# Stacked Q and K rows of the attention stages filled from SBUF in twelve DMAs of eight rows

## The reference

```python
q = split_heads(x @ wq + bq); k = split_heads(c @ wk + bk); v = split_heads(c @ wv + bv)
attn = softmax(einsum('bhqd,bhkd->bhqk', q, k) / sqrt(8))
out = einsum('bhqk,bhkd->bhqd', attn, v)        # heads joined again
y = out @ wo + bo
```

## Time and profile before

| | |
|---|---|
| Median of 3 runs | 6247.15 us (6244.76 to 6252.29) |
| Span of the profiled execution | 6237.0 us |
| Stage X | 2609 to 3357 us |
| Attention of F | 3357 to 4083 us |
| Stage N | 4487 to 5284 us |
| Stage Y | 5284 to 5992 us |
| TensorE, VectorE, ScalarE, GpSimd busy | 73%, 72%, 45%, 48% of the span |
| DMA | 420.18 MB, 67 GB/s in the mean |

### The profile page before, as it was taken

How to read it: one execution, slowest core, us unless ns; L and a number is a source line. 1 busy time by engine, 2 the same in 40 slices (tenths; PEclk the granted TensorE clock), 3 DMA queues, 4 the chain that set the end, 5 groups by cost and what they waited for, 6 DMA issues and landing times. The chain is left out here.

```text
span 6237.0 us, 103921 instructions
## 1 busy us (share of the span) xinstructions
PE 4570.7 (73%) x29564; PEld 3083.8 (49%) x29564; DVE 4491.5 (72%) x8773; ACT 2792.4 (45%) x6405; POOL 2994.0 (48%) x2850
## 2 busy tenths in 40 slices
PE   5777777777777777488885888846468777678853
PEld 2333333333233333266664777745367776677731
DVE  6999999999999999677776555543456655344468
ACT  4555555555555555265663333345534333233334
POOL 6777777777777777544443111144511112111102
PEclk8988989999898999799997899968778888899965
DMA  2111111111111111144442444441243442444320
GB/s 73 58 60 60 60 60 60 60 60 60 60 60 60 59 60 58 30 78 76 78 76 52 86 87 81 81 131 55 89 75 72 81 75 56 77 76 73 72 48 27
DMA packets 319745, 420.18 MB, mean 67 GB/s; under 512 B 39955, under 2 KB 301286, under 8 KB 308710
## 3 DMA queue, kind: packets, MB, share of 16 engines
q1 hardware_dynamic: 315110, 408.16, 27.9%
q0 software_dynamic: 4352, 8.95, 0.4%
HBM read 307.46 MB, written 109.58 MB: 67 GB/s over the span
## 5 line engine op out<-in xcount | busy, mean ns | idle before, releaser
L2162 POOL TENSOR_TENSOR m_h<-m_dtu,m_Bb 128x512 f32<-128x512 f32 x1024 | 1587.2, 1579 | 234.0 <-PE bank L1797 228.2
L1797 PE MATMUL bank<-m_h,ident 128*128 128x512 f32 x2048 | 1214.4, 684 | 498.5 <-DVE m_h L2061 485.7
L1797 PEld LDWEIGHTS bank<-m_h,ident 128*128 128x128 f32 x2048 | 364.4, 207 | 1162.4 <-DVE m_h L2061 1007.0
L2055 DVE TENSOR_TENSOR_SCAN m_h<-m_dA,m_h 128x512 f32<-128x512 f32 x512 | 749.2, 1463 | 6.2 <-DVE m_sz L1988 6.2
L2061 DVE TENSOR_TENSOR m_h<-m_h,bank 128x512 f32<-128x512 f32 x1024 | 671.7, 656 | 4.9 <-DVE m_h L2055 2.7
L2055 DVE TENSOR_TENSOR_SCAN m_h<-bank,m_h 128x512 f32<-128x512 f32 x512 | 620.3, 1212 | 28.1 <-DVE m_sz L1988 11.7
L385 PE MATMUL bank<-x_pT,x_vB 128*64 128x128 f32 (+1 forms) x4096 | 583.5, 288 | 9.2 <-ACT x_ou L520 9.2
L1944 ACT ACTIVATE bank<-m_dt,m_A 128x512 f32<-128x512 f32 x512 | 352.3, 688 | 492.2 <-DVE m_h L2055 434.8
L1944 ACT ACTIVATE m_dA<-m_dt,m_A 128x512 f32<-128x512 f32 x512 | 367.2, 717 | 429.1 <-DVE m_h L2055 425.4
L385 PEld LDWEIGHTS bank<-x_pT,x_vB 128*64 128x64 f32 (+1 forms) x4096 | 466.9, 147 | 58.9 <-issue 49.3
L511 ACT ACTIVATE x_sm<-x_sm,x_nm 128x77 f32<-128x77 f32 x1024 | 353.2, 348 | 123.1 <-DVE x_nm L673 123.0
(11 more groups left out here) (425 smaller groups left out, 11010.0 us busy)
## 6 DMA issues: line engine op xcount, KB each, us to landing
m_Bb<-m_B SPq DMA_DIRECT2D x32, 4096.0 KB, 11.9
x_Ks<-x_k_parts SPq DMA_DIRECT2D x32, 462.0 KB
x_q_parts<-x_qp SPq DMA_DIRECT2D x32, 384.0 KB, 2.5
x_Qs<-x_q_parts SPq DMA_DIRECT2D x32, 384.0 KB
f_Ks<-f_k_parts SPq DMA_DIRECT2D x16, 768.0 KB
a_Ks<-a_k_parts SPq DMA_DIRECT2D x16, 768.0 KB
x_xp<-x_stage SPq DMA_DIRECT2D x32, 256.0 KB
x_Qs<-x_q_parts SPq DMA_DIRECT2D x32, 256.0 KB
```

The costliest lines, as they stand in the source:

```text
L1797: pe.matmul(banks[4 + c], ident[:], h[:, k % RING, :], start=(s == 0), stop=(s == NS - 1)).then_inc(s_ya.sem, 1)
L2055: v.tensor_tensor_scan(h[:, k % RING, :], decays[k % AHEAD], h[:, k % RING, :], 0.0, ALU.mult, ALU.add).then_inc(s_h.sem, 1)
L2162: pool.tensor_tensor(h[:, k % RING, :], dtu[:, d, c, :], Bb[:, d, s, :], ALU.mult).then_inc(s_dB.sem, 1)
```

## The change

`stack` no longer writes to DRAM. As soon as Q's low part is there (and the readers of the old stack are done) SP issues six DMAs, each of which copies one part of `qp` (128 partitions of 512 columns) into one block of eight rows of `Qs`; when K's low part is there it issues six more into `Ks`. The semaphore `s_stk` becomes two, one for Q and one for K, each complete after six DMAs. TensorE waits for both. VectorE's `high` and GpSimd's `low` now wait for the stack fills of the group before, since these read `qp`. The saves, their semaphore and the DRAM tensors are gone. `Q_ORDER` and `K_ORDER` name the part of each block; the contents of the stacks are the same.

```diff
--- before.py
+++ after.py
@@ -80,6 +80,8 @@
     kt = GB * sk
     PARTS, ROWS = 3, 6 * DH
     K_TIMES = (3, 2, 1)
+    Q_ORDER = (0, 1, 2, 0, 1, 0)
+    K_ORDER = (0, 0, 0, 1, 1, 2)
     VC = DH + (gate is None)
     VW = 8 * VC
     TURNS = NG // 2
@@ -115,9 +117,6 @@
 
         def sem(name, per=1):
             return Count(nc.alloc_semaphore(f"{tag}_{name}"), per)
-
-        dram_q = nc.dram_tensor(f"{tag}_q_parts", (2, PARTS, P, GT), BF16, kind="Internal").ap()
-        dram_k = nc.dram_tensor(f"{tag}_k_parts", (2, sum(K_TIMES), P, kt), BF16, kind="Internal").ap()
 
         w = sb("w", [P, 4, D])
         bqk = sb("bqk", [P, 2])
@@ -164,7 +163,7 @@
         s_xpfree = sem("x_used"); s_pb = sem("proj_written", NU); s_pf = sem("proj_evacuated", NU)
         s_hi = sem("hi_ready", 2); s_r1 = sem("rest1_ready", 2)
         s_mid = sem("mid_ready", 2); s_lo = sem("lo_ready", 2)
-        s_ps = sem("parts_stored", 16 * (PARTS + 1)); s_stk = sem("stack_loaded", 16 * (PARTS + 1))
+        s_stk = [sem(f"stack_loaded{t}", 16 * sum(K_TIMES)) for t in range(2)]
         s_ln = sem("front_var", 1); s_lp = sem("front_pow", 1); s_xn = sem("front_norm", 1)
         s_neg = sem("neg_ready"); s_sq = sem("squares", 2); s_ms = sem("sums_of_squares", 2); s_rt = sem("roots"); s_qn = sem("qk_normed", 2)
         s_S = sem("scores", 4); s_Sf = sem("scores_used", 4); s_nmp = sem("max_parts"); s_T = sem("max_transposed")
@@ -232,26 +231,14 @@
                     sp.dma_start(gp[:, par], gate.rearrange("(g b) t d -> g t b d", b=GB)[g]).then_inc(s_gp[par].sem, 16)
 
             def stack(g, par):
-                def save(dst, src):
-                    sp.dma_start(dst.rearrange("a p t -> p a t"), src).then_inc(s_ps.sem, 16)
-
-                def fill(stack_rows, parts):
-                    sp.dma_start(stack_rows.rearrange("p h t -> p (h t)"),
-                                 parts.rearrange("a (d h) t -> (a d) (h t)", d=DH)).then_inc(s_stk.sem, 16)
-                sp.wait_ge(s_lo.sem, s_lo.at(g, 1))
-                save(dram_q[par], qp[:, 0])
-                sp.wait_ge(s_lo.sem, s_lo.at(g, 2))
-                at = 0
-                for part, times in enumerate(K_TIMES):
-                    save(dram_k[par, at:at + times], qp[:, 1, part:part + 1, 0:kt].to_broadcast([P, times, kt]))
-                    at += times
-                sp.wait_ge(s_ps.sem, s_ps.at(g + 1))
-                sp.wait_ge(s_use.sem, s_use.at((g - 1) * GB))
-                at = 0
-                for parts in K_TIMES:
-                    fill(Qs[at * DH:(at + parts) * DH, par], dram_q[par, 0:parts])
-                    at += parts
-                fill(Ks[0:ROWS, par], dram_k[par])
+                def fill(t, stacked, at, part, n):
+                    sp.dma_start(stacked[at * DH:(at + 1) * DH, par], qp[:, t, part, 0:n]).then_inc(s_stk[t].sem, 16)
+                for t, stacked, n, order in ((0, Qs, GT, Q_ORDER), (1, Ks, kt, K_ORDER)):
+                    sp.wait_ge(s_lo.sem, s_lo.at(g, t + 1))
+                    if t == 0:
+                        sp.wait_ge(s_use.sem, s_use.at((g - 1) * GB))
+                    for at, part in enumerate(order):
+                        fill(t, stacked, at, part, n)
 
             def residual(g, par):
                 sp.wait_ge(s_store.sem, s_store.at((g - 1) * 16))
@@ -334,7 +321,8 @@
             def scores(i, lb, c):
                 b, l, q = 8 * i + lb, lb // GB, lb % GB
                 if c == 0 and q == 0:
-                    pe.wait_ge(s_stk.sem, s_stk.at(2 * i + l + 1))
+                    for t in range(2):
+                        pe.wait_ge(s_stk[t].sem, s_stk[t].at(2 * i + l + 1))
                 pe.wait_ge(s_Sf.sem, s_Sf.at(b, c + 1 - 2))
                 for h in range(4):
                     hh = 4 * c + h
@@ -623,7 +611,7 @@
 
             def high(v, ch, g, t):
                 n = (GT, kt)[t]
-                v.wait_ge(s_ps.sem, s_ps.at(g))
+                v.wait_ge(s_stk[t].sem, s_stk[t].at(g))
                 v.wait_ge(s_pf.sem, s_pf.at(g, nu[(Q, K)[t]] + 1))
                 v.tensor_copy(qp[:, t, 0, 0:n], qf[:, t, 0:n]).then_inc(s_hi.sem, 1)
 
@@ -814,7 +802,7 @@
             def low(g, t):
                 n = (GT, kt)[t]
                 pool.wait_ge(s_mid.sem, s_mid.at(g, t + 1))
-                pool.wait_ge(s_ps.sem, s_ps.at(g))
+                pool.wait_ge(s_stk[t].sem, s_stk[t].at(g))
                 pool.wait_ge(s_r1.sem, s_r1.at(g, t + 1))
                 pool.tensor_tensor(qp[:, t, 2, 0:n], qr[:, t, 0:n], qp[:, t, 1, 0:n], ALU.subtract).then_inc(s_lo.sem, 1)
```

## The result

| | before | after |
|---|---|---|
| Median | 6249.24 us (4 runs, 6244.76 to 6252.29) | 6476.76 us (4 runs, 6473.84 to 6484.74) |
| Span of the profiled execution | 6237.0 us | 6477.6 us |
| Mean granted clock of TensorE | 0.859 | 0.845 |

The ratio is 1.0366 with a 95% interval of 1.0351 to 1.0380: slower by 228 us, by 240.6 us in the profiled spans. The forecast was slower, 6580 us, with a range from 6370. Sign and mechanism were right; the growth was forecast too large, by 91 us against the spans and by 104 against the medians. The forecast also put 10.15 us around the span. In the profiled execution after, 2.0 us lie there (6479.64 us with a span of 6477.6), so most of the 10 us was the difference between one execution of the kernel before and its median.

What follows compares the result with a forecast made beforehand. The prediction took whole-core bubbles at TensorE's first score matmul, waiting for slow stack fills, as the bound. Span 6237.0 us plus 332 us of longer chains plus 10.15 us around it gave 6579, rounded to 6580 us; range 6370 to 6860.

Steps and rivals of the forecast that it cites:

- The reading of the bound: TensorE's first score matmul waits for K-stack fills, 374.7 us in all; each wait idles the whole core, 60 times plus stage starts.
- (1): Removing one Q save, three K saves and their landing wait per group takes 6.1 us out of F's chain.
- (2): Twelve added fills into eight rows each cost 2.41 us per 128 KB, between bounds of 0.81 (or 0.41) and 2.60 us.
- u: Time of one 128 KB fill into eight rows, forecast 2.41 us, ranged from 2.15 to 2.8 us.
- rival A: Faster: slow fills come from reading 16 KB DRAM pieces, not the destination; all waits go, about 5800 us; chance 0.13.
- (3): Chain from Q's parts to scores after the change: 29.9 us in F and N, 24.15 us in X and Y.
- (4): Growth per group F +7.4, N +7.0, X +1.0, Y +4.9; with first groups +332 us, as a function 691u - 1334.
- (5): Waits for old stack readers, now ahead of Q fills and the K wait, and "high" and "low" waits cost nothing.
- (6): SP issues twelve DMAs instead of eight, 4.3 us, hidden under 29 us of transfer; residual load has 4 us to spare.
- Rival C: Slower: SP's queue backs up by 8.77 us, delaying store and residual in F, +77 us, 6656 us; chance 0.14.
- (7): TensorE's clock after a bubble is 0.50 already; a longer bubble ends in the same 0.50, adding nothing.
- B: No change: u near 1.93 us, where starting 6.1 us earlier just pays for slower writing; chance 0.03.

Runs made afterwards that it cites:

- run 4: The kernel before, saves and DRAM source kept, its fills cut into twelve DMAs of eight neighbouring rows: 6709.08 us, ratio 1.0733 against before.
- run 6: The changed kernel with the six fills of each stack issued in block order 0, 4, 1, 5, 2, 3: 6567.44 us, ratio 1.0497 against before.
- run 1: The changed kernel with the eight destination rows of each fill twelve partitions apart instead of neighbouring: 5709.96 us, ratio 0.9145 against before.
- run 3: The kernel before, DRAM round trip and four fills kept, with all stacked rows two partitions apart: 5909.39 us, ratio 0.9453 against before.
- run 8: The changed kernel with only each group's first Q fill cut in two, rows 0 to 5 and 6 to 7: 6202.62 us, ratio 0.9905 against before.
- run 5: The changed kernel with the loads of x, context, mask and gate issued ahead of the twelve fills: 6453.25 us, ratio 1.0304 against before.
- run 2: The changed kernel with the eight destination rows of each fill two partitions apart: 5773.79 us, ratio 0.9236 against before.

## Why the prediction was right in direction and too high

**The reading of the bound** held. A bubble of the whole core at this line, 60 times and once at each stage's start: the waits grew by 238.6 us and the span by 240.6.

**(1) The saves removed, 6.1 us of the chain.** Right: SP issues the Q fills where it issued the Q save, and their first packet moves 1.3 us behind it in F, where it was 6.9 before. With the same twelve fills the round trip costs 232 us (run 4 against after), 3.6 us for each of 64 groups; it is less than 6.1 since the fills from DRAM are quicker by 3.3 us in F, 3.4 in X and 1.9 in Y.

**(2) The price of a fill, u = 2.41 us.** This is the term that was mis-sized. In F it was 2.17 us, in N 1.96, in X and Y 2.0 to 2.1 for a Q fill (medians of 12.6 and 12.2 us for six). The rate while fills alone run was as forecast, 57 to 60 GB/s against "50 to 60", in F; it is 65 in N. The assumption that failed is the last one of that step, that "the fills follow one another": run 6 speaks against it, since the fills' order alone moves the time by 1.3%, and in F the first engine ends its part of a fill 0.8 us before the last, which leaves it free for the next fill. That the destination sets the price, which step (2) took over rival A, is what runs 1, 3 and 4 show.

**(3) The chain, 12u + 1.0.** The constant was too small: the fills begin 1.25 us after they are issued, and TensorE resumes 2.0 us behind their last packet, 3.2 together (1.29 and 1.92 as medians over F). The two errors have opposite signs. In F, 12 x 2.17 + 3.2 = 29.2 against the forecast 29.9, and so they hide each other; in N, 12 x 1.96 + 3.2 = 26.7 against 29.9.

**(4) The sum.** Forecast +332, measured +232 in the chains. The chains after, by the means in the table, are shorter than forecast by 3.5 us in N, 1.4 in Y, 1.1 in F and 0.6 in X: 6.6 x 15 = 99 us, and that is the miss, half of it in N. The chains before, taken from one group each, were right to half a microsecond, and their errors cancel. So what cost most was one u for four stages: nothing in the trace before told N from F. That the time still fell well inside the range owes something to luck, since N's u of 1.96 is below the 2.15 that the range went down to and the constant made up for it: by the forecast's own function the growth of 228 us is u = 2.26.
In F's fourth group the chain was 24.1 us and in N's last 21.9, with the same DMAs, and there the bursts are gone as in run 8 (0.60 and 0.49 us in the table above): the engines had lost step. In both a 16 KB piece of an instruction fetch passes through the DMA engines 4.5 us behind the first issue and takes 1.8 to 1.9 us. That it put them out of step is argued, not shown; F's second, third and fifth groups have such pieces at other times, of 1.0 to 1.2 us, and take 29.1 to 29.4 us. In N the bursts are a little looser than in F (1.17 against 1.44 us of pause), which goes with the quicker fills; why is open.

**(5) The moved waits cost nothing.** Right: the rest of a group is within 0.2 us of what it was in every stage.

**(6) SP.** The count was right and the price too low: twelve issues take 3.92 + 5.22 = 9.1 us, not 4.3, since each of the first six takes about 0.65 us, and the load behind them takes 2.74 instead of 0.4 us (3.69 in X). It hardly reaches the end: run 5, which takes these loads from behind the fills, gains 0.6%. The residual load was issued at 3534.75, 1.3 us after the scores resumed, and VectorE never waited for it. Rival C did not happen.

**(7) The clock.** Right for the change as made: TensorE's busy time is 4573.3 against 4570.7 us. The bubble of the group shown doubled (6.75 to 13.45 us), and the half-clock work behind it did not grow. But rival A's estimate of half a microsecond a bubble was too small by a factor of more than four: when the bubbles go, 2.3 us a group come back (run 1).

**The rivals.** A is refuted as a reading of the trace (run 3). Its picture of a kernel whose fills are fast came true only with spread rows, at 5710 us, below its 5800 because of the clock. B's zero at u = 1.93 us is nearly what N showed, 1.96, and N was slower by 3.5 us a group all the same: with 3.2 us for the constant the zero lies lower, 22.9 = 12u + 3.2 or u = 1.64 us in N.

## What to carry to other kernels

Before a round trip through DRAM is taken out, look at what the transfer on the end of the chain writes to: here the fills into a few neighbouring partitions were the long part before, and cutting them into pieces of eight rows made it longer (22.4 us instead of 14.1 in F, run 4). Where the rows of a stack are free to choose, spread those of one DMA over the partitions; with one index expression changed this gave the fastest kernel here, 5710 us, 8.6% under the kernel before and 11.8% under the change as made. And count a bubble of TensorE as more than its wait: with it goes a stretch at half clock behind it, here 2.3 us a group by run 1.

## What was not expected of the hardware

- Eight neighbouring rows take 57 to 65 GB/s from SBUF in 1 KB pieces, and 55 from DRAM in 16 KB pieces in the window shown; at every second row it is 117, at every twelfth 168 GB/s (windows above, fills alone).
- The engines that carry out such fills end them in step, in bursts of eight with pauses of 1.44 us in F, and lose step by one uneven cut: then the same bytes into the same rows take 20.4 us in F instead of 26.0.
- The order of the same twelve DMAs is worth 1.3%, and one uneven cut in one of them (6 + 2 rows) against an even one (4 + 4) 5.8% of the time before (ratios 0.9905 and 1.0488).
- From the last packet of the fills to TensorE's start 1.9 us pass in F and N of after, 1.3 in F of run 2, and 0.9 to 1.0 in F and N of the kernel before (medians).
- SP's issue of one such DMA takes about 0.65 us (3.92 us for six), against 0.36 for a fill from DRAM in the earlier trace rows. Behind the slow fills it takes longer: 5.22 us for the six K fills in F, where run 1 needs 3.96.
